# First self attention in two halves of the tokens, with context attention between the pieces of the second half

## The reference

```python
# self attention ("power"): each batch of T = 256 tokens by itself, 8 key heads, 2 query heads for each, head size 128
logG = cumsum(log_sigmoid(x @ Wg + 6.906768))
a    = tril(((q @ k.T) / sqrt(128)) ** 2 * exp(logG[t] - logG[s]))
y    = (a @ v) / (sum(a) + 1e-6)
x    = layernorm(x + y @ Wc + bc)
# context attention: 16 heads of 32, causal softmax over the batch's 256 context rows,
# no weights: query = x, key = value = ctx
p    = softmax(tril(x_h @ ctx_h.T / sqrt(32)))
x    = layernorm(x + concat_h(p @ ctx_h))
```

## Time and profile before

| | |
|---|---|
| median of 3 runs | 2402.16 us (2396.13 to 2412.57) |
| profiled execution | span 2397.8 us from first to last instruction; the page gives no other time of it |
| busy | PE 89%, PEld 71%, DVE 53%, ACT 41%, POOL 29% |
| granted TensorE clock, mean | 0.930 of 2.4 GHz |
| transfers | 86.45 MB, mean 36 GB/s |
| one query and key weight transfer | 768 KB, 5.9 us to landing, 8 of them |
| one output weight transfer | 512 KB, 4.5 us, 8 of them |

### The profile page before, as it was taken

One profiled execution on the slowest core, in us unless ns is written; L12 is line 12 of the kernel. 1 busy time (PEld: TensorE's weight loads), 2 busy tenths in 40 slices (PEclk: granted clock), 3 DMA queues, 4 the chain that ended last, 5 costly groups with the idle time before them and its releaser, 6 DMA issues.

```text
span 2397.8 us, 37028 instructions
## 1 busy us (share of the span) xinstructions
PE 2137.6 (89%) x13669; PEld 1705.2 (71%) x13669; DVE 1263.5 (53%) x3237; ACT 993.1 (41%) x2275; POOL 689.1 (29%) x633
## 2 busy tenths in 40 slices
PE   7899999999997898788999999978999868888774
PEld 6789889889885666577888888865656356666542
DVE  2654554553557666554111123346777676777556
ACT  3322322332324766432211211235566647777632
POOL 2832332332331111103443410044454331322110
PEclk9999999999997866599999999989999889999986
DMA  3210110100001110101010000024233310000001
GB/s 140 86 41 22 34 40 17 38 28 26 28 13 54 36 37 10 41 18 36 27 53 18 18 27 1 1 40 63 49 55 56 99 41 25 17 19 6 1 10 71
DMA packets 41730, 86.45 MB, mean 36 GB/s; under 512 B 6224, under 2 KB 20816, under 8 KB 38736
## 3 DMA queue, kind: packets, MB, share of 16 engines
q1 hardware_dynamic: 41552, 84.08, 12.6%
HBM read 63.55 MB, written 4.26 MB: 28 GB/s over the span
## 4 chain that ended last, share of the span: by engine, by line
PE 39%; issue 14%; DVE 8%; ACT 5%; POOL 3%; DMA 1%; SPq 0%; DVEq 0%; ACTq 0%; POOLq 0%
PE PS L1136 14%; PE PS L1208 4%; PE PS L1235 3%; PE PS L1619 3%; PE PS L1715 3%; DVE aM L1852 2%; ACT xP L2377 1%; PE PS L1683 1%; DVE st L137 1%; PE PS L2229 1%; POOL xN L1021 1%; PE PS L1670 1%; PE PS L1703 1%; DVE PS L2499 1%; PE PS L1726 1%
## 5 line engine op out<-in xcount | busy, mean ns | idle before, releaser
L1136 PE MATMUL PS<-WH,bXH 128*128 128x512 f32 x512 | 201.0, 392 | 5.4 <-POOL WL L1429 5.4
L1136 PE MATMUL PS<-WL,bXH 128*128 128x512 f32 x512 | 200.4, 391 | 0.0
L1136 PE MATMUL PS<-WH,bXL 128*128 128x512 f32 x512 | 200.3, 391 | 0.0
L1339 DVE SCALAR_TENSOR_TENSOR s<-s,cf,PS 128x256 f32<-128x256 f32 x112 | 53.9, 481 | 249.0 <-ACT s L1254 240.0
L1852 DVE TENSOR_REDUCE aM<-PS 128x4 f32<-128x1024 f32 x128 | 153.8, 1222 | 57.9 <-PE PS L1683 56.9
L1254 ACT ACTIVATE s<-PS 128x256 f32<-128x256 f32 x128 | 49.3, 385 | 278.7 <-PE PS L1136 278.5
L307 PE MATMUL PS<-aXH,QKH 128*128 128x512 f32 x384 | 154.0, 401 | 0.0
L307 PE MATMUL PS<-aXH,QKL 128*128 128x512 f32 x384 | 151.6, 395 | 0.0
L307 PE MATMUL PS<-aXL,QKH 128*128 128x512 f32 x384 | 151.5, 395 | 0.0
L1791 ACT ACTIVATE aPT<-PS 128x1024 f32<-128x1024 f32 x128 | 128.4, 1024 | 49.6 <-PE PS L1703 48.8
L506 ACT ACTIVATE sq<-PS 128x768 f32<-128x768 f32 x64 | 52.0, 813 | 210.1 <-PE PS L397 163.5
(11 more groups left out here) (406 smaller groups left out, 6112.6 us busy)
## 6 DMA issues: line engine op xcount, KB each, us to landing
lgB<-gate_sums SPq DMA_DIRECT2D x32, 256.0 KB, 3.6
sg<-in_gu SPq DMA_DIRECT2D x8, 1024.0 KB, 4.8
aqs<-aQH SPq DMA_DIRECT2D x64, 128.0 KB, 4.1
gQK<-in_Wqk SPq DMA_DIRECT2D x8, 768.0 KB, 5.9
xN<-in_xT SPq DMA_DIRECT2D x4, 1024.0 KB, 10.4
gC<-in_Wc SPq DMA_DIRECT2D x8, 512.0 KB, 4.5
xN<-in_x SPq DMA_DIRECT2D x4, 1024.0 KB, 7.2
cst<-in_cT SPq DMA_DIRECT2D x8, 512.0 KB, 4.7
```

The lines of the kernel that those rows point to most:

```text
L1136: mm = e.matmul(PS[:, b, :], x[:, kc, 128 * t:128 * t + 128], w[:, kc, :], start=kc == 0 and i == 0, stop=kc == KC - 1 and i == 2)
```

## The change

- `steps` runs both groups of 1024 tokens one after the other: for each half h, all 8 groups g, and for each of them the two parts 2h and 2h+1. A group's weights now serve two steps; query and key weights and output weights are fetched and split 16 times, not 8, value weights 7 times, not 4 (`events`). XH, XL and V are split by half; those of the first half lie in the SBUF region that the context attention uses later.
- Every stage function of these two stages is now a generator, cut into ticks. `in_order` runs the ticks of all stages in one list `order`, the same for every engine and for the bank plan. A step n of the self attention has 8 ticks: project m = 0, 1, 2; out 0 and 1; out 2 and 3; attend (and values); scores; turn.
- Steps 0 to 16 run alone. From step 17 to step 33 two ticks of the context attention follow each four of the self attention, until 66 are done; the rest runs after the self attention. Its ticks count from -8; tick 16j + 2i is scores and softmax of pair i of batch j, the next its transposes.
- From step 17 the self attention has banks 0 to 3 only; the context attention has 4 and 5 for scores, 6 and 7 for all else, in the inside part and after it.
- The context attention has one buffer for KH, KL, QH, QL, cst, V, PT and nT, and a P for one pair of heads; PT is always copied by ACT. Key, query and V are fetched and split in parts (halves, quarters).
- Norms use one of two sets of small tiles (`Space`), so that those of both stages can be under way together; the last four tiles' norm of the self attention ends in that stage. Semaphore names are shared more widely.

The loops over ticks below are, in this order, PE's, ACT's and SP's of the context attention; its `attend(j, g)` waits for the PT copies of both its pieces (f_out), its `flip(j, i)` for the exponentials of piece i (s_exp).

```diff
-    steps = [(g, p) for g in range(8) for p in range(NP)]
+    steps = [(g, 2 * h + p) for h in (0, 1) for g in range(8) for p in (0, 1)]
+    events = {0: 0, 4: 1, 8: 2, 12: 3, 20: 4, 24: 5, 28: 6}
+    tiles_of = [range(NT)] + [range(0, 8)] * 3 + [range(8, 16)] * 3
...
+            among = (0, 8 if n < alone else 4)
...
+def in_order(order, pieces):
+    for s, n in order:
+        for _ in range(n):
+            next(pieces[s])
...
-        P = [W(f"cP{i}", [128, 4, 3, 128]) for i in range(2)]
-        PT = [W(f"cPT{i}", [128, 4, 384]) for i in range(2)]
+    PT, P = W("cPT", [128, 4, 384]), W("cP", [128, 2, 3, 128])
+    first, last = -8, 16 * J + 8
...
+    def batch(tick, lag):
+        j, r = (tick - lag) // 16, (tick - lag) % 16
+        return (j, r) if 0 <= j < J else (0, -1)
...
+            if r >= 0 and r % 2 == 0:
+                R.use(("c_s", j, r // 2), 2, s_exp.upto(8 * j + r // 2 + 1), among=(4, 6))
+            elif r >= 0:
+                R.use(("flip", j, r // 2), 2, f_out.upto(8 * j + r // 2 + 1), among=(6, 8))
...
+        for tick in range(first, last):
+            j, r = batch(tick, 4)
+            if r >= 0 and r % 4 == 0:
+                attend(j, r // 4)
+            j, r = batch(tick, 0)
+            if r >= 0 and r % 2 == 0:
+                scores(j, r // 2)
+            elif r >= 0:
+                flip(j, r // 2)
+            j, r = batch(tick, 18)
+            if r == 0:
+                finish(j)
+            for i, lag in enumerate((-6, 6)):
+                j, r = batch(tick, lag)
+                if r == 0:
+                    turn(j, i)
+            yield
...
+            if r >= 0 and r % 2 == 0:
+                b = rooms["c_s", j, i][0]
+                if n:
+                    e.wait_ge(*f_in.upto(n))
...
+            elif r >= 0:
+                b = rooms["flip", j, i][0]
+                if n >= 2:
+                    e.wait_ge(*a_mm.upto(n // 2))
+                e.wait_ge(*f_in.upto(n + 1))
+                e.activation(PT[:, 2 * (i % 2):2 * (i % 2) + 2, :], PS[:, b:b + 2, 0:384], ACTF.Copy).then_inc(f_out.sem, 1)
...
+            j, r = batch(tick, 5)
+            if r >= 0 and r % 4 == 0 and j + 1 < J:
+                g = r // 4
+                e.wait_ge(*a_mm.upto(4 * j + g + 1))
+                e.dma_start(V[:, :, 128 * g:128 * g + 128],
+                            d["c"][:, 2 * j + 2:2 * j + 4, 128 * g:128 * g + 128]).then_inc(in_v[g].sem, 16)
...
+        a0 = attention0(K, 17)
+        c0 = cross0(K)
...
+        A, C, done = 1, 2, 0
+        order = [(0, 1), (A, 1 + 8 * 17)]
+        for n in range(17, 34):
+            for ticks in (4, 4):
+                beside = min(2, 66 - done)
+                order += [(A, ticks), (C, beside)]
+                done += beside
+        order += [(A, 2), (C, c0.ticks - done)]
+        order += [(i, 1) for i in range(3, 7)]
```

More of the change, by code:

```diff
@@ L49, in __init__, with take @@
         self.age, self.left, self.held, self.now, self.of = list(range(-8, 0)), [()] * 8, [False] * 8, 0, {}
-    def take(self, key, n=1, pack=False):
-        starts = [s for s in range(0, 8, n) if not any(self.held[s:s + n])]
+    def take(self, key, n=1, pack=False, among=(0, 8)):
+        starts = [s for s in range(among[0], among[1], n) if not any(self.held[s:s + n])]
         b = min(starts, key=lambda s: (pack and n == 1 and not self.held[s ^ 1], max(self.age[s:s + n])))
@@ L62, in give, with use @@
             self.held[i], self.left[i], self.age[i] = False, left, self.now
-    def use(self, key, n, *left, pack=False):
-        self.take(key, n, pack)
+    def use(self, key, n, *left, pack=False, among=(0, 8)):
+        self.take(key, n, pack, among)
         self.give(key, n, *left)
@@ new lines, in tensor, with project @@
+    def tensor(e):
+        def project(n, m):
+            g, p = steps[n]
+            b, left = rooms["qk", n, m]
+            for w in left:
+                e.wait_ge(*w)
+            if m == 0:
+                e.wait_ge(*qk_hi.upto(n // 2 + 1))
+                e.wait_ge(*qk_lo.upto(n // 2 + 1))
+            c = 512 * (p % 2)
+            for kc in range(KC):
+                for i, (w, x) in enumerate(pair3((QKH, XH[p // 2]), (QKL, XL[p // 2]))):
+                    mm = e.matmul(PS[:, b, :], w[:, kc, 128 * m:128 * m + 128], x[:, kc, c:c + 512],
+                                  start=kc == 0 and i == 0, stop=kc == KC - 1 and i == 2)
+            mm.then_inc(qk_mm.sem, 1)
@@ L609, in vector @@
                                     ALU.subtract).then_inc(t_lo.sem, 1)
[L610 to L612 removed]
+            norm(n, 7)
+            yield
+        norm(N + 2, 0)
+        yield
+        yield
     def gpsimd(e):
@@ new lines, in sync @@
+            if n in events and events[n] < 6:
+                v = events[n]
+                e.wait_ge(*v_hi.upto(v + 1))
+                e.wait_ge(*(v_lo.upto(v) if v else v_lo0.upto(1)))
+                e.dma_start(gV[:, :, 0:256], d["Wv"][(0, 1, 2, 3, 1, 2, 3)[v + 1]]).then_inc(in_v.sem, 16)
+            yield
+            yield
+            yield
+        yield
+        yield
+    K.first_half = qk_mm.upto(3 * 16), v_mm.upto(before[4]), y_mm.upto(2 * 16)
+    K.ends = (o_mm.upto(4 * N), t_hi.upto(2 * N), o_add.upto(4 * N), e_in.upto(2 * N), c_lo.upto(16), norms[NP - 1].done.upto(4))
@@ L1040, in experts0 @@
+    K.ends += (n_mm.upto(2 * J), a_out.upto(4 * J), n_out.upto(2 * J), added.upto(2 * J), n_rec.upto(J))
+    return Stage(last - first, banks, tensor, scalar, vector, gpsimd, sync)
 def experts0(K):
```

1048 lines of the change are left out of this document (527 added, 521 removed).

## The result

The changed kernel takes 2654.43 us (median of 4 runs, 2648.72 to 2661.41), the one before 2402.16: ratio 1.1054, 95% interval 1.1005 to 1.1104. The forecast was 2639, range 2525 to 2690. Rows of the page after: span, busy times, the granted clock in 40 slices, and the costliest group (busy us, mean ns, idle time of the engine ahead of it and its releaser).

A forecast was written before the change was run, and what follows sets the result against it. TensorE was taken to bound self attention (busy all of 100 us), with room on paper in context attention. Inside 228 + alone 252 - old stage 243 = +237 us on the median 2402.16: 2639 us, range 2525 to 2690.

The forecast's parts named there:

- The wait in the block: Inside self attention, flip waits for its scores' exponentials: 15 blocks after out at 4.09 us, 14 after turn at 6.63, 154 us.
- The clock inside: Inside self attention, matmuls behind each block's wait run slow: 47 us, 35 for long blocks and 12 for short ones.
- short ones half: Slow matmuls behind the 15 short blocks, after out, charged at half of 1.7 us each; long ones, after turn, fully.
- The bound of 60: Inside self attention, slow matmuls charged behind every block: 15 x 1.7 + 14 x 2.5 = 60 us.
- Four banks: Self attention has only banks 0 to 3 from step 17; waiting for `out` banks costs 0.8 us a step, 12 us.
- Drain: At self attention's end, late pieces fill PE's idle 5.87 + 1.86 us: 8 us taken off.
- Halves: Weights fetched and split more often for halves of the tokens; hidden by 11.0 us of other PE work, costed at nothing.
- Alone: The 35 pieces after self attention, with chain, products, turns and finishes: 185 us upper clock level, 260 lower; 252 taken.
- nine tenths low: In the 35 pieces alone, the clock is taken as nine tenths at the lower level, giving 252 us.
- The clock did not hold: Rival that the clock holds its upper level: 181 inside and 185 alone, +123, 2525 us; chance 0.2.
- starvation by SyncE or weights: Rival: SyncE tied to PE's progress, or context norms on VectorE, makes each second step late: +40, 2680 us; chance 0.15.
- the faster rival: Maxima and exponentials done before PE reaches flip: 69 us inside, 133 for the rest, -41, 2361 us; chance 0.03.

The follow-up runs named there:

- one_tick: Changed kernel with one piece of context attention after every two pieces of self attention, the flip a quarter step behind its scores: 2528.40 us, 1.0506.
- apart: Changed kernel with no context attention inside self attention, which keeps all eight banks; all 64 pieces run after it: 2642.47 us, 1.0987.
- apart_4: Changed kernel with no context attention inside self attention, which still keeps to four banks from step 17: 2670.59 us, 1.1124.
- best6: Changed kernel with single-piece insertion, a fifth self-attention bank, overlap restored for pieces alone, and there ScalarE's next exponentials before its copy: 2413.48 us, 1.0049.

## Why the prediction was right, step by step

**The wait in the block.** Forecast 4.09 and 6.63 us a block; the step shown has 4.85 and 6.76. The way to the flip was right in both (3.69 and 5.62 us against 3.45 and 5.99). The flip itself was mis-sized: I priced six transposes at 0.64, the upper level, but in most blocks they ran at the lower level and took 1.16. The 29 blocks of the trace take 174 us with the turns and finishes inside them, where 154 + 11 = 165 stood: 13 more for the flips, 4 less for the rest. one_tick shows that this wait is the cause: with the flip moved away from its scores, 131 us of waiting and slow matmuls go.

**The clock inside.** Forecast 47 us. The groups of TensorE of the changed kernel from 380 to 992 (busy us, mean ns, idle time), then of apart to 760:

```profile
L384 PE MATMUL PS<-aXH,QKH 128*128 128x512 f32 x192 | 84.9, 442 | 3.8 <-ACT sq L597 3.4 <-DVE yL L722 0.4
...
L417 PE MATMUL PS<-CH,yH 128*128 128x512 f32 x147 | 69.9, 475 | 3.4 <-DVE qkL L684 3.4
...
L958 PE MATMUL PS<-idF,cP 128*128 128x128 f32 x174 | 41.3, 405 | 107.9 <-ACT cP L1032 96.1 <-DVE coN L1087 11.9
```

```profile
L384 PE MATMUL PS<-aXH,QKH 128*128 128x512 f32 x192 | 76.1, 396 | 0.0
...
L417 PE MATMUL PS<-CH,yH 128*128 128x512 f32 x145 | 58.5, 403 | 10.0 <-issue 10.0
```

The projection has three such groups, 246.6 us together against 225.8: 21 us. The output products have 200.2 against 173.9 at nearly the same count: 24 us at equal count. The sum, 45, is close to the forecast by luck, since two sizes were wrong in opposite directions: I charged 2.5 us behind a long block and 0.85 behind a short one, and both cost about 1.5 us on average. The step that failed is "short ones half". With the flips' 13 us the clock costs 58.

My reading of the earlier trace rows, that a short gap leaves part of the burst fast, was true but priced wrongly. What stays fast is the front of the burst, and the slow part comes behind it. A short block of the trace, and a wait for a bank in the first step with four banks:

```profile
959.55 0.85 PE L958 MATMUL PS<-idF,cP 128*128 128x128 f32 x6 [2.74 <-ACT cP L1032]
...
960.87 0.63 PE L417 MATMUL PS<-CH,yL 128*128 128x512 f32 x1
...
432.47 0.50 PE L384 MATMUL PS<-aXH,QKH 128*128 128x512 f32 x1 [2.73 <-ACT sq L597]
```

In four of the 15 short blocks the flip takes 0.60 to 0.74 us to the next matmul instead of 1.16, and slow matmuls (0.63, against 0.39 at the upper level) come behind it. Likewise in the earlier trace rows only the two or three matmuls from 748.25 on are fast; from 749.05 to 752.03 they take 0.63. But behind the wait of 2.73 us at 432.47 the next matmuls take 0.40 and 0.39 and the granted clock stays at 1.00: the length of a wait alone does not decide.

The bound of 60 beside the forecast went by the Trainium skill ("TensorE: Matmul & The Clock Gate", section "HAM oscillation — how this bites in real kernels"), which tells of a kernel whose waits, of some 3 to 5 us, each throttle the next burst. The trace agrees in kind, and for shorter waits too: slow matmuls follow the wait in all 29 blocks, the shortest of 2.74 us. That the size, 58, is so near 60 is luck, as the bound did not hold the flips' 13 us and charged the matmuls behind the blocks 60 where they cost 45.

**Banks, drain, halves.** Four banks: 12 forecast, some 4 in the changed kernel (3.8 us ahead of L384), probably because waits for exponentials let the banks come free; without insertions they cost 28 (apart_4), and with the waits for exponentials gone 17 from 400 to 760 us (one_tick). The edit was priced in the wrong surroundings. Drain: -8 forecast; the idle time ahead of L417 fell from 10.0 to 3.4, -7. Halves: 0 forecast, 5 measured, at the kernel's start alone, where the second weights come half as many steps after the first and the cover that I named does not hold yet: TensorE did wait once in the projection for weights, 2.90 us. Together: 174 + 11 products + 1 for the first turn + 45 + 4 - 7 + 5 = 233, with 236.6 in the trace and 228 in the forecast.

**Alone.** 263.6 us against 252. The forecast's bound for all at the lower level was 260, and the clock is 0.50 from 998 us to the end of it: "nine tenths low" gave away 8 us. The rest is the join, whose norm on VectorE and ScalarE no term of mine held: 9.68 us where a piece's wait has 2.74, so 7 us, offset by pieces a little quicker than charged. Of the signs that I had named, TensorE's busy share there is 57%, not under half, and a piece costs 7.53 us, just over the 7.5 named.

**The rivals.** The clock did not hold (2525), and apart from that one wait of 2.90 us no starvation by SyncE or weights is in TensorE's waits from 400 to 1256 us. The mechanism of the faster rival, exponentials done before TensorE reaches the flip, is what one_tick brings about; there the 29 pieces cost 861.1 - 760.7 = 100.4 us, 3.5 each, where the rival had 69 with everything else in it. It did not pay since 35 pieces alone still took 7.5.

**What the sum hid.** My terms priced the insertion well but did not say that it earned nothing: apart, with none, is 12 us faster. The loss splits better so: 64 pieces in the new form, (7.48 - 3.80) x 64 = 235; halves 5; the insertion 12.

## What to carry to other kernels

Work put into a full engine's stream did not pay here while its own dependent halves stood together: put the producer in one slot and the consumer in the next. Before trading an overlapped stage for another arrangement, price the pieces that stay outside without their double buffers; here a second buffer and their old order were worth 100 of the 252 us. An edit that frees a bank or a wait is worth what the surroundings leave of it: a fifth bank gained 11 us inside and lost 18 alone, where its users shared a pair; without that sharing it gained 12 by the medians.

## What the runs showed of the hardware

- Waits of 2.74 to 2.87 us between stretches of dense 512-column matmuls (the 15 short blocks) were each followed by matmuls at the lower level, 1.4 us lost on average. In eleven the first six transposes were already slow, in four the slow matmuls came later. A wait of 2.73 us at 432.47 had none behind it.
- With waits of some 2.7 and 1.0 us in the pieces the granted clock stayed at 0.50 for some 260 us, and for 480 us in apart, though TensorE was 57% busy.
- Being busy did not by itself bring it back: 19.46 of 20 us busy at 0.50 in best6, 18.92 of 20 in the kernel before, both in small transposes, 32-row matmuls and products with the context. What would have brought it back there wasn't tried, and stays open.
- Adding 22 matmuls of no use in the wait of each piece made the kernel 53 us faster.
